# Products that nobody reads on TensorE, from the first router's search to the attention stage

## The chip, the cores and the metric

The kernel runs on one core of one Trainium2 chip. The metric is the device time of one execution in microseconds. Before the change three runs gave 2144.35, 2140.17 and 2142.94 us, median 2142.94 us. The change is judged by the time of the changed kernel against that.

## The reference

The program is a small language-model tower of two layers. For this case only the front of layer 0 matters: tokens are embedded, mixed by a recurrence, normalised, and then a router with 4 experts picks, per sequence and expert, the 256 of 512 tokens with the highest probability. The picks set which bands of columns each token uses in the attention and feed-forward layer behind it.

```python
    h = _L0_tok_ref(x, L0_tok_W)
    h = h + _L0_attn_ref(_layernorm(h, axis=-1), ...)          # recurrence
    h = h + _L0_ffn_ref(_layernorm(h, axis=-1), ...)           # router, attention, MLP
    ...
def _L0_ffn_ref(x, w_router, ...):
        cap = int(CAP_FACTOR * N)                              # 256 of 512
        logits = jnp.einsum('bnc,ec->bne', x, w_router)
        probs = jax.nn.softmax(logits, axis=-1)
        gate, idx = jax.lax.top_k(jnp.swapaxes(probs, 1, 2), cap)
        ...
        attn = jax.nn.softmax(jnp.einsum('bhqd,bhkd->bhqk', q, k) * scale, axis=-1)
```

## The kernel before, in words

The kernel is a chain of phases. Each phase is one block in which every engine has its own written-out program, and semaphores order them. Between two phases stands a barrier: each engine runs a DRAIN and then raises the barrier's semaphore (line 45), GpSimd releases all, SyncE clears the semaphores of the phase one after the other (line 53), and a second barrier (line 49) lets the next phase begin. No engine starts the next phase before the slowest has come to the barrier.

The first phase, `embed_and_route`, ends with the router. TensorE transposes the probabilities to 32 rows (8 sequences by 4 experts) of 512 tokens (line 636). VectorE copies them (line 504) and searches the 256th largest value of each row bit by bit, in `kth_largest`: 30 steps, each a comparison with a count over 512 columns (line 146), a decision (line 148) and the new candidate (line 150), with a drain behind each. TensorE has nothing to do meanwhile; its next instruction waits for `taken_ready`. VectorE then marks the ties and forms the two rows of taken tokens (lines 508 to 519), TensorE transposes them in 8 small matmuls (line 641), and VectorE spreads them into the tile `bands` (lines 526 and 528). That is the phase's last work.

The next phase, `moe_attention_ffn`, begins for GpSimd with the scaling of `y` by `bands` (line 910). TensorE's first work is the transposes of `y` (line 1110, 8 matmuls, two groups of four, each read out by ScalarE at line 1300), then three tiles of queries and keys (line 1120) and six tiles of the MLP (line 1135), each two calls of 512 columns in f32, then the values (line 1127). Only then come the row maxima of the attention (line 1145), which need `qT` and `c_kT`; these are loaded through DRAM by SyncE's queue (lines 853, 863 and 866) after VectorE has split each tile of queries and keys into three bf16 parts (lines 955 to 965). VectorE gets to the first split behind a memset of one row of `c_kT` (line 1068). The row maxima then alternate between TensorE and VectorE (line 975).

Of the kernel before, what the change touches and what calls it, by code (L numbers as in the profile page):

```python
# [5 lines left out]
ALU = mybir.AluOpType  # L6
# [128 lines left out]
CAP0 = T // 2  # L135
BANDS = ((0, 24), (24, 48), (48, 96), (96, 192))
TOP_BIT = 29
QUARTS = (TOP_BIT + 1) // 2

def kth_largest(dve, scores, cand, drop, count, mark, k):

    dve.memset(cand[:, :], 1 << TOP_BIT)
    dve.drain()
    for b in range(TOP_BIT, -1, -1):
        dve.tensor_scalar(mark, scores, cand[:, :].bitcast(F32), 0.0, ALU.is_ge, ALU.add, accum_out=count[:, :])
        dve.drain()
        dve.tensor_scalar(drop[:, :], count[:, :], float(k), float(1 << b), ALU.is_lt, ALU.mult)
        dve.drain()
        dve.scalar_tensor_tensor(out=cand[:, :], in0=cand[:, :], scalar=(1 << b) >> 1, in1=drop[:, :],  # L150
                                 op0=ALU.bitwise_or, op1=ALU.bitwise_xor)
        dve.drain()

# [44 lines left out]
def embed_and_route(kit, a, x1, bands, dealt, moe, work, spare):  # L199
# [6 lines left out]
    with kit.phase() as ctx:  # L206
# [29 lines left out]
        x1T = sb("b_xT", [P, 2, 2, T])  # L236
# [3 lines left out]
        bits = sb("bits", [R, 1], I32)  # L240
        drop = sb("drop", [R, 1], I32)
        count = sb("count", [R, 1])
        room = sb("room", [R, 1])
        ps_w = ps("a_ps_w", [P, BANKS_A, T])
        ps_o = ps("a_ps_o", [P, 4, T])
# [5 lines left out]
        score, mark, tie = (pnum[0:R, i, 0:T] for i in range(3))  # L251
# [8 lines left out]
            "a_small_in a_w_loaded a_rows_ready a_folded a_zeroed a_cleared a_var_ready a_rstd_ready a_xn_ready a_w_psum "  # L260
            "a_w_read a_met a_gaps_ready a_exps_ready a_z_ready a_out_psum a_h_done a_x1_ready a_den_ready a_logit_psum "
            "a_logit_read")
        shifted, exp_ready, probs_ready, score_psum, taken_ready, taken_psum = kit.sems(
            "b_shifted b_exp_ready b_probs_ready b_score_psum b_taken_ready b_taken_psum")
        moe_in, y_var, y_rstd, y_norm, y_scaled = kit.sems("a_moe_in a_y_var a_y_rstd a_y_norm a_y_scaled")
        rows_in = [kit.pool_dma_sem(f"a_rows_in{n}") for n in range(PAIRSEQ)]
        order = front_order()
# [69 lines left out]
        def _(dve):  # L337
# [165 lines left out]
            dve.wait_ge(score_psum, 1)  # L503
            dve.tensor_copy(score, ps_w[0:R, 0, :])
            dve.drain()
            kth_largest(dve, score, bits, drop, count, mark, CAP0)
            kth = bits[:, :].bitcast(F32)
            dve.tensor_scalar(mark, score, kth, 0.0, ALU.is_gt, ALU.add, accum_out=count[:, :])
            dve.tensor_scalar(tie, score, kth, None, ALU.is_equal)
# [22 lines left out]
        def _(pe):  # L532
# [102 lines left out]
            for j in range(J):  # L635
                last = pe.transpose(ps_s[:, j, :], prob_rows[:, j].rearrange("p b e -> p (b e)"), kit.ident[:, :])
            last.then_inc(score_psum, 1)
            pe.wait_ge(taken_ready, 1)
            for w in range(2):
                for j in range(J):  # L640
                    last = pe.transpose(ps_b[:, w, j, :], taken[:, w, j * P:(j + 1) * P], kit.ident[0:R, 0:R])
            last.then_inc(taken_psum, 1)

        @block.scalar
        def _(act):
# [2284 lines left out]
def lm_tower(nc, a, out_rows):  # L2930
    out = out_rows.rearrange("(b p) c -> p b c", p=P)
    dealt = nc.dram_tensor("dealt", (SLOTS, CX), F32, kind="Internal").ap()
    spread = nc.dram_tensor("spread", (G3, P, 3, T), BF16, kind="Internal").ap()
    with ExitStack() as ctx:
        kit = Kit(nc, ctx)
        setup_constants(kit)
        if PHASES > 1:
            ssm = SsmInputs(tile_maker(nc, ctx))
            with ExitStack() as layer:
                sb = tile_maker(nc, layer)  # L2940
                x1 = sb("x1", [P, NB, C])
                bands = sb("bands", [P, 2, NB, EXPERTS0])
                moe = MoeInputs(sb)
                embed_and_route(kit, a, x1, bands, dealt, moe, ssm.xm, ssm.w_in)
                moe_attention_ffn(kit, a, x1, bands, moe, ssm, spread)
        if PHASES > 2:
            state_space_block(kit, a, ssm)
        if PHASES > 3:
            experts_tower(kit, a, dealt, out, out_rows)
        else:  # L2950
            store_output(kit, out)
# [81 lines left out]
```

## Time and profile before

| what | before |
|---|---|
| median of three runs | 2142.94 us |
| the profiled execution, whole | 2141.69 us |
| its span, first to last instruction | 2139.8 us |
| mean granted TensorE clock | 0.939 |
| TensorE busy, matmuls | 1932.6 us, 90% of the span |
| VectorE busy | 1152.7 us, 54% |
| ScalarE busy | 739.9 us, 35% |
| GpSimd busy | 425.5 us, 20% |

The profiled execution is one run; it took 1.25 us less than the median and lies 1.89 us above its own span. Busy shares are means over stages with different limits, so they do not say what a change in one stage is worth.
### The profile page before, as it was taken

The page shows a single profiled execution, that of the slowest core. Times are in us where ns is not written, and L with a number is a line of the kernel's source. Part 1 is how long each engine was busy: PE and PEld are TensorE (multiplying, and loading weights), DVE is VectorE, ACT ScalarE, POOL GpSimd, SP SyncE. Part 2 cuts the span into 40 slices and gives each one's busy share as a digit, 9 for nine tenths or more (in the row PEclk, how much of TensorE's full clock was granted, in tenths as well). Part 3 has the DMA queues.
Part 4 walks back from the last instruction along what each step waited for, and adds up shares of the span by engine and source line. Part 5 has one row for each costly group of instructions (what it writes and reads, how often), then busy time and mean ns, then how long its engine had stood idle before and what let it go on. Part 6 is the DMA issues. An engine that isn't in the chain of part 4 may idle for free. (4 is left out here: it accounts for less than half of the span.)

```text
span 2139.8 us, 27931 instructions
## 1 busy us (share of the span) xinstructions
PE 1932.6 (90%) x10040; PEld 1216.2 (57%) x10048; DVE 1152.7 (54%) x2714; ACT 739.9 (35%) x1248; POOL 425.5 (20%) x521
## 2 busy tenths in 40 slices
PE   4997609999999999879999998799999999999997
PEld 2343503345444444445666665465558888888886
DVE  5798577676667665456877885347322222222221
ACT  1434002544555455544555553121111111111111
POOL 5200201120222021111111111100561222222222
PEclk9998557999999999978999999699999999999998
DMA  2610002211111112010000000200222322122221
GB/s 63 222 50 0 0 18 74 60 52 53 45 52 53 52 39 59 1 31 6 6 6 6 8 9 1 100 1 1 75 88 70 68 59 60 32 62 61 68 39 18
DMA packets 68746, 94.72 MB, mean 44 GB/s; under 512 B 15386, under 2 KB 57662, under 8 KB 66337
## 3 DMA queue, kind: packets, MB, share of 16 engines
q1 hardware_dynamic: 52482, 77.19, 11.2%
q0 software_dynamic: 16128, 15.76, 4.2%
q8 instruction: 80, 1.31, 0.3%
q14 instruction: 56, 0.46, 0.1%
HBM read 54.96 MB, written 39.47 MB: 44 GB/s over the span
## 5 line engine op out<-in xcount | busy, mean ns | idle before, releaser
L975 DVE TENSOR_REDUCE row_max<-c_ps_m 128x1 f32<-128x512 f32 x384 | 252.6, 686 | 114.2 <-PE c_ps_m L1145 108.9
L1323 ACT ACTIVATE e<-c_ps_s 128x512 f32<-128x512 f32 x384 | 216.6, 596 | 222.0 <-PE c_ps_s L1161 221.3
L2622 DVE TENSOR_TENSOR e_f<-e_ps_u,e_gate 128x512 f32<-128x512 f32 x120 | 83.0, 691 | 271.6 <-ACT e_gate L2904 179.1
L2423 POOL DMA_INDIRECT out<-m_o,m_row_of x80 | 125.7, 1572 | 280.7 <-issue 260.3
L2839 PE MATMUL e_ps_o<-m_w,e_f 128*128 128x192 f32 x960 | 162.6, 326 | 0.9 <-DVE e_f L2622 0.9
L2839 PEld LDWEIGHTS e_ps_o<-m_w,e_f 128*128 128x128 f32 x960 | 158.1, 190 | 3.3 <-DVE e_f L2622 1.3
L1145 PE MATMUL c_ps_m<-c_kT,qT 96*128 96x512 bf16 x384 | 150.2, 398 | 10.7 <-DVE row_max L975 10.6
L1161 PE MATMUL c_ps_s<-qT,c_kT 97*128 97x512 bf16 x384 | 145.4, 389 | 12.7 <-ACT e L1323 5.0
L2904 ACT ACTIVATE e_gate<-e_ps_g 128x512 f32<-128x512 f32 x120 | 71.7, 597 | 242.3 <-PE e_ps_g L2813 162.3
L2807 PE MATMUL e_ps_g<-m_xT,m_w 128*128 128x256 f32 x480 | 129.6, 392 | 1.0 <-DVE h L2454 1.0
L2807 PE MATMUL e_ps_u<-m_xT,m_w 128*128 128x256 f32 x480 | 123.2, 379 | 0.0
L2817 PE MATMUL e_ps_u<-m_xT,m_w 64*128 64x256 f32 x480 | 119.5, 389 | 0.0
L2813 PE MATMUL e_ps_g<-m_xT,m_w 64*128 64x256 f32 x480 | 119.5, 389 | 0.0
L1172 PE MATMUL c_ps_a<-e,v 128*32 128x512 f32 x768 | 106.3, 626 | 1.0 <-ACT e L1323 1.0
L2813 PEld LDWEIGHTS e_ps_g<-m_xT,m_w 64*128 64x128 f32 x480 | 85.0, 186 | 27.9 <-issue 19.9
L2807 PEld LDWEIGHTS e_ps_g<-m_xT,m_w 128*128 128x128 f32 x480 | 83.1, 190 | 28.4 <-issue 19.9
L2807 PEld LDWEIGHTS e_ps_u<-m_xT,m_w 128*128 128x128 f32 x480 | 91.2, 190 | 12.4
L1161 PEld LDWEIGHTS c_ps_s<-qT,c_kT 97*128 97x128 bf16 x384 | 36.5, 97 | 107.3 <-ACT e L1323 82.3
L2630 DVE TENSOR_SCALAR m_o<-e_ps_o,m_w_of 128x192 f32<-128x192 f32 x80 | 29.7, 413 | 125.8 <-PE e_ps_o L2839 125.8
L1135 PE MATMUL c_ps_w<-yT,w 96*128 96x512 f32 x192 | 90.3, 596 | 0.0
L2397 POOL DMA_INDIRECT dealt<-e_x,slot x64 | 62.5, 977 | 116.6 <-issue 111.0
L2817 PEld LDWEIGHTS e_ps_u<-m_xT,m_w 64*128 64x128 f32 x480 | 85.0, 186 | 0.0
(440 smaller groups left out, 3704.4 us busy)
## 6 DMA issues: line engine op xcount, KB each, us to landing
dealt<-x SPq DMA_DIRECT2D x8, 1290.0 KB, 15.0
m_x<-dealt SPq DMA_DIRECT2D x40, 258.0 KB, 2.7
spread<-parts SPq DMA_DIRECT2D x24, 384.0 KB, 2.3
qT<-spread SPq DMA_DIRECT2D x144, 64.0 KB, 2.5
c_kT<-spread SPq DMA_DIRECT2D x144, 64.0 KB, 2.4
m_w<-in_w13e SPq DMA_DIRECT2D x8, 1152.0 KB, 5.2
m_w<-in_w2e SPq DMA_DIRECT2D x8, 576.0 KB, 6.3
out<-h SPq DMA_DIRECT2D x8, 384.0 KB, 4.6
```

The lines of the kernel that those rows point to most:

```text
L975: dve.tensor_reduce(row_max[:, n // J, n % J:n % J + 1], ps_m[:, n % 2, :], AX_X, ALU.max)\
L1135: last = pe.matmul(bank(key), w1[0:CH + c, c, m * P:(m + 1) * P], yT[0:CH + c, c, :], start=c == 0, stop=c == 1)
L1145: pe.matmul(ps_m[:, n % 2, :], qT[0:STACK, h, j * P:(j + 1) * P], kT[0:STACK, h, :], start=True, stop=True).then_inc(m_psum, 1)
L1161: pe.matmul(ps_s[:, n % 2, :], kT[:, h, kc * P:(kc + 1) * P], qT[:, h, :], start=True, stop=True).then_inc(s_psum, 1)
L1172: last = pe.matmul(ps_a[32 * i:32 * i + 32, :], v[:, t % 2, kc, 4 * g + i, :], e[:, (4 * grp + i) % LIVE_E, :], start=kc == 0, stop=kc == ...
L1323: act.activation(e[:, n % LIVE_E, :], ps_s[:, n % 2, :], ACT.Exp, scale=QSCALE).then_inc(e_ready, 1)
L2423: pool.indirect_dma_start(out=out_rows, out_offset=bass.IndirectOffsetOnAxis(ap=row_of[:, n % 2, r:r + 1], axis=0), in_=o[:, n % 2, r, :], ...
L2622: dve.tensor_tensor(fe[:, n % 2, 2 * i:2 * i + 2, :], ps_ue[:, q % 2], gate_e[:, q % 2], ALU.mult)\
L2807: last = pe.matmul(dst[:, q % 2, k, :], w13e[:, u, w, here[k]], xeT[:, b, 0, :], start=first and k == 0, stop=not first and k == 1, skip_g ...
L2813: g_last = pe.matmul(ps_ge[:, q % 2, k, :], w13e[0:HALF, u, 2, here[k]], xeT[0:HALF, b, 1, :], start=first and k == 0, stop=not first and ...
L2817: u_last = pe.matmul(ps_ue[:, q % 2, k, :], w13e[HALF:P, u, 2, here[k]], xeT[HALF:P, b, 1, :], start=first and k == 0, stop=not first and ...
L2839: last = pe.matmul(ps_oe[:, b, r, 0:C], fe[:, b, m, r * P:(r + 1) * P], w2e[:, u, m, :], start=m == 0, stop=m == IT - 1)
```

## The change

Each step of the search now raises a new semaphore, `step`, from its last VectorE instruction. TensorE gets work that writes to the free tile `ps_o`, which nobody reads afterwards: at each of the 30 steps one product of the identity with 512 columns of `x1T`, f32, and six at the last step; and six more behind the transposes of the taken rows, before TensorE's end of the phase. The phase has one semaphore more to clear.

```diff
-def kth_largest(dve, scores, cand, drop, count, mark, k):
+def kth_largest(dve, scores, cand, drop, count, mark, k, step):
...
         dve.scalar_tensor_tensor(out=cand[:, :], in0=cand[:, :], scalar=(1 << b) >> 1, in1=drop[:, :],
-                                 op0=ALU.bitwise_or, op1=ALU.bitwise_xor)
+                                 op0=ALU.bitwise_or, op1=ALU.bitwise_xor).then_inc(step, 1)
...
             last.then_inc(score_psum, 1)
+            for n in range(TOP_BIT + 1):
+                pe.wait_ge(step, n + 1)
+                for i in range(6 if n == TOP_BIT else 1):
+                    pe.matmul(ps_o[:, i % 4, :], kit.ident[:, :], x1T[:, 0, 0, :], start=True, stop=True)
             pe.wait_ge(taken_ready, 1)
             for w in range(2):
                 for j in range(J):
                     last = pe.transpose(ps_b[:, w, j, :], taken[:, w, j * P:(j + 1) * P], kit.ident[0:R, 0:R])
             last.then_inc(taken_psum, 1)
+            for i in range(6):
+                pe.matmul(ps_o[:, i % 4, :], kit.ident[:, :], x1T[:, 0, 0, :], start=True, stop=True)
```

TensorE's instructions of the kernel before, from the transposes of the probabilities to the first transposes of `y`. `a_ps_w` and `a_ps_o` are PSUM tiles of the first phase, `c_ps_w` one of the second, `qden` holds the taken rows; each row is one form with its count.

```order
373 L636 MATMUL a_ps_w<-ident,fresh 32x128 [waits b_probs_ready,a_w_read]
374 L636 MATMUL a_ps_w<-ident,fresh 32x128 x3
375 L641 MATMUL a_ps_w<-ident,qden 128x32 [waits b_taken_ready]
376 L641 MATMUL a_ps_w<-ident,qden 128x32 x7
377 L45 UNCONDITIONAL_BRANCH
378 L1098 UNCONDITIONAL_BRANCH [waits barrier_Pool_Activation_PE_DVE_SP_release]
379 L1110 MATMUL c_ps_w<-ident,y 96x128 [waits c_y_ready]
```

In it TensorE goes from one wait straight to the next, and the 8 transposes are the last thing before the barrier. The same stretch of TensorE's program in the changed kernel, where `b_xT` is the tile `x1T` and lines behind the change stand 4 to 6 further:

```order
373 L636 MATMUL a_ps_w<-ident,fresh 32x128 [waits b_probs_ready,a_w_read]
374 L636 MATMUL a_ps_w<-ident,fresh 32x128 x3
375 L641 MATMUL a_ps_o<-b_xT,ident 128x512 [waits b_step] x30
376 L641 MATMUL a_ps_o<-b_xT,ident 128x512 x5
377 L645 MATMUL a_ps_w<-ident,qden 128x32 [waits b_taken_ready]
378 L645 MATMUL a_ps_w<-ident,qden 128x32 x7
379 L648 MATMUL a_ps_o<-b_xT,ident 128x512 x6
380 L45 UNCONDITIONAL_BRANCH
381 L1104 UNCONDITIONAL_BRANCH [waits barrier_Pool_Activation_PE_DVE_SP_release]
382 L1116 MATMUL c_ps_w<-ident,y 96x128 [waits c_y_ready]
```

35 products now stand ahead of the transposes of the taken rows, 30 of them behind a wait of their own, and six between those transposes and the barrier. The order on the other engines is as it was.

## Rows read from the trace of the kernel before

**Rows 1.** The page: span, and granted clock in 40 slices.
```profile
span 2139.8 us, 27931 instructions
PEclk9998557999999999978999999699999999999998
```
**Rows 2.** Timeline, VectorE, search, first and last of 30 steps (start, duration, engine, line).
```profile
266.39 0.73 DVE L146 TENSOR_SCALAR_CACHE_REDUCE pnum<-pnum,bits 32x512 f32<-32x512 f32 x1
...
303.29 0.73 DVE L146 TENSOR_SCALAR_CACHE_REDUCE pnum<-pnum,bits 32x512 f32<-32x512 f32 x1
...
304.32 0.15 DVE L150 SCALAR_TENSOR_TENSOR bits<-bits,drop 32x1 int32<-32x1 int32 x1
```
**Rows 3.** Timeline, from the taken rows to the next phase.
```profile
309.80 1.06 PE L641 MATMUL a_ps_w<-ident,qden 32*128 32x32 f32 x8 [44.38 <-DVE qden L518]
...
314.85 1.93 POOL L910 TENSOR_TENSOR y<-y,bands 128x96 f32<-128x96 f32 x4 [64.27 <-POOLq L49]
...
316.97 1.94 PE L1110 MATMUL c_ps_w<-ident,y 128*96 128x128 f32 x8 [6.11 <-POOL y L911]
```
**Rows 4.** Barrier, lines 45 and 53: count, shortest/median/longest ns, first to last start.
```profile
L45 PEldq DRAIN  x1: 1088/1088/1088, 309.8 to 309.8; - x1
L45 DVEq DRAIN  x1: 19/19/19, 312.5 to 312.5; - x1
...
L53 SPq EVENT_SEMAPHORE_RANGE_CLEAR  x32: 25/30/39, 312.7 to 314.5; - x32
```
**Rows 5.** End of the attention phase: TensorE's last matmuls (timeline), its DRAIN (line 45).
```profile
917.30 0.81 PE L1209 MATMUL c_ps_w<-w_att,xaT 96*128 96x192 f32 x4
...
L45 PEldq DRAIN  x1: 3117/3117/3117, 915.0 to 915.0; - x1
```
**Rows 6.** Pauses of TensorE: windows (busy us and counts, clock, DMA), one timeline row.
```profile
39.20:43.88 4.68, 0.00 (x0) 0.00 (x0) 4.38 (x18) 1.08 (x2) 3.27 (x4) 0.94 0.00 0
...
43.88 2.82 PE L544 MATMUL a_ps_w<-ident,xn 128*128 128x128 f32 x12 [4.70 <-DVE xn L129]
...
46.80:50.00 3.20, 3.20 (x8) 1.16 (x7) 3.03 (x4) 0.54 (x1) 2.59 (x3) 1.00 0.30 53
...
147.66:149.43 1.77, 0.01 (x1) 0.04 (x1) 1.61 (x2) 1.77 (x4) 0.00 (x0) 1.00 0.07 30
...
918.12:923.11 4.99, 0.00 (x0) 0.03 (x1) 1.88 (x6) 0.02 (x1) 0.00 (x0) 0.75 0.01 2
```
**Rows 7.** Window of the attention phase's first 512-column matmuls.
```profile
319.60:326.65 7.05, 7.05 (x9) 2.92 (x10) 6.70 (x4) 1.25 (x1) 0.00 (x0) 0.50 0.00 0
```
**Rows 8.** Weight loads of neighbouring matmuls (timeline); all matmuls of line 1135.
```profile
323.18 0.34 PEld L1120 LDWEIGHTS c_ps_w<-yT,w 96*128 96x128 f32 x1 [0.52 <-issue]
...
324.03 0.34 PEld L1120 LDWEIGHTS c_ps_w<-yT,w 97*128 97x128 f32 x1 [0.52 <-issue]
...
L1135 PE MATMUL c_ps_w<-yT,w x24: 590/592/687, 328.3 to 338.3; 96*128 96x512 f32 x12, 97*128 97x512 f32 x12
```
**Rows 9.** Ahead of the row maxima (timeline), and landing times (page, last number).
```profile
319.77 5.18 DVE L1068 MEMSET c_kT<- 1x6144 bf16 x1 [1.32 <-issue]
...
336.51 0.43 SPq L866 DMA_DIRECT2D c_kT<-spread  x1
...
341.37 0.59 PE L1145 MATMUL c_ps_m<-c_kT,qT 96*128 96x512 bf16 x2
...
c_kT<-spread SPq DMA_DIRECT2D x144, 64.0 KB, 2.4
```
**Rows 10.** Timeline, VectorE: line 957 raises a semaphore, 955 does not; drains between.
```profile
324.96 0.69 DVE L955 CAST parts<-c_ps_w 128x512 bf16<-128x512 f32 x1
325.73 0.69 DVE L957 TENSOR_TENSOR rest<-c_ps_w,parts 128x512 f32<-128x512 f32 x1
...
326.51 0.43 DVE L963 CAST parts<-rest 128x512 bf16<-128x512 f32 x1
```
**Rows 11.** Windows of the first row maxima.
```profile
343.80:347.10 3.30, 2.26 (x6) 0.55 (x6) 3.30 (x6) 0.00 (x0) 0.00 (x0) 1.00 0.52 141
347.20:350.00 2.80, 2.42 (x4) 0.42 (x4) 2.59 (x5) 0.00 (x0) 0.00 (x0) 0.50 0.45 130
```

More of the change, by code:

```diff
@@ L262, in embed_and_route @@
             "a_logit_read")
-        shifted, exp_ready, probs_ready, score_psum, taken_ready, taken_psum = kit.sems(
-            "b_shifted b_exp_ready b_probs_ready b_score_psum b_taken_ready b_taken_psum")
+        step, shifted, exp_ready, probs_ready, score_psum, taken_ready, taken_psum = kit.sems(
+            "b_step b_shifted b_exp_ready b_probs_ready b_score_psum b_taken_ready b_taken_psum")
         moe_in, y_var, y_rstd, y_norm, y_scaled = kit.sems("a_moe_in a_y_var a_y_rstd a_y_norm a_y_scaled")
@@ L505, in _ @@
             dve.drain()
-            kth_largest(dve, score, bits, drop, count, mark, CAP0)
+            kth_largest(dve, score, bits, drop, count, mark, CAP0, step)
             kth = bits[:, :].bitcast(F32)
```

## The prediction

> **What bounds the kernel now.** I read the page first. Its clock row is lowest, at 5, in the fifth and sixth slice (214 to 321 us), and the sixth is where the change works [rows 1]. Then I read the timeline from the search on. The search is VectorE's alone: 30 steps, from 266.39 to 303.29 in 29 intervals, so 1.27 us each, the last ending at 304.32 + 0.15 = 304.47 us [rows 2]. TensorE sits idle for 44.38 us until the taken rows are there, does its 8 transposes in 1.06 us, and idles again for 6.11 us [rows 3]. Nothing that TensorE does before 309.8 is waited for, so the phase's end is set by VectorE, and a faster TensorE can gain at most the transposes there.
>
> The view of the barrier shows how the phase ends. VectorE's DRAIN at 312.5 us takes 19 ns and is the last to arrive; the next phase starts at 314.85 [rows 3, 4]. TensorE's DRAIN begins at 309.8, before its transposes are through, and lasts 1088 ns, to 310.90, which is where the last of them ends (309.80 + 1.06 = 310.86).
>
> In the next phase TensorE does work that is waited for. Its 512-column matmuls begin at 319.60 and run at the granted clock 0.50 until 326.65 [rows 7], 1.2 GHz, start to start 324.03 - 323.18 = 0.85 us; behind that they are (338.3 - 328.3) / 23 = 0.435 us apart [rows 8], 2.4 GHz. The first row maximum starts at 341.37 [rows 9], right behind TensorE's own queue, so what this stretch saves or loses goes to the end, up to the point where another wait is later: the loads for the maxima, the last issued at 336.51 and landing some 2.4 us later, at 338.9 [rows 9]. These loads hang on VectorE's splits, which begin only behind the 5.18 us memset (to 324.95), so they do not come earlier with a faster TensorE. The margin is 341.37 - 338.9 = 2.5 us.
>
> **The search with products.** One f32 product of 512 columns is two matmuls in the trace: line 1135 makes 6 x 2 = 12 calls and has 24 rows [rows 8]. It takes 2 x 0.85 = 1.70 us at half clock and 2 x 0.435 = 0.87 us at full. At half clock TensorE falls behind the 1.27 us steps and works without a pause; at full clock it catches up and is idle for 0.40 us in each step. VectorE never waits for it. The last step releases six products: 12 x 0.435 = 5.22 us from 304.47, so to 309.69, and the taken rows come at 309.80 [rows 3]. So nothing is late there, at full clock.
>
> The search itself gains nothing. Its price is the semaphore: an instruction that raises one ends at 325.73 + 0.69 = 326.42 and the next starts at 326.51, a gap of 0.09 us, and behind one that raises none the gap is 325.73 - 325.65 = 0.08 [rows 10]. Over 30 steps the difference is 0.3 us; bounds 0 and 0.6. It delays TensorE's end as much as VectorE's.
>
> **The end of the phase.** The transposes run at full clock: half of (1.06 - 0.29) / 7 = 0.11 us each, so 8 x 0.055 = 0.44 us, and VectorE gets them 0.4 us sooner. That gain is covered, because TensorE is now the last to arrive. Its six products are 12 x 0.435 = 5.22 us from 309.80 + 0.44 = 310.24, so to 315.46, with 0.16 us until the last one is through (a duration of 0.59 against a distance of 0.435 [rows 8]) and 0.05 for the DRAIN: 315.67. The barrier waited until 312.5. The delay is 3.17 us, with the 0.3 us of the search 3.47, and with one more clear of (314.5 - 312.7) / 31 = 0.06 us [rows 4] it is 3.5 us. Everything in the next phase hangs behind this barrier: GpSimd's scaling, SyncE's loads, VectorE's memset. Bounds: 3.2 if the semaphore is free, 3.8 if it costs double.
>
> **The clock after the barrier.** TensorE stands still from 315.6 to 316.97 + 3.5 = 320.5, 4.8 us. Of pauses in this trace, one of 4.68 us and one of 4.99 us each lost the full clock before they were over (means 0.94 and 0.75 inside them), and one of 1.77 us kept it [rows 6]. So the attention phase starts at half clock again. How long it stays there is open: before, 7.05 us of 512-column work [rows 7]; after the 4.68 us pause the clock was back some 2.9 us after work resumed, at 46.8 [rows 6]. In our case 2.6 us go by on transposes and a wait first (316.97 to 319.60), so the half-clocked 512-column work is between 0.3 and 7.05 us, and half the difference to 7.05 is saved: 0 to 3.4 us, cut to 2.5 by the loads. The nearest row is the same stretch before, which gives 0. I take 1.0, a little toward the other end.
>
> The Trainium skill has a rule on this: TensorE: Matmul & The Clock Gate, Part 4: PE-mode transpose, says that transposes do not count as busy work for the clock. By that rule the transposes at the head of the attention phase would bring nothing back, and the sum would be the full 3.5 us. The trace disagrees in one place: 12 transposes, from 43.88 to 46.70, were nearly all that TensorE had done since its pause when it had full clock again at 46.8 [rows 6]. By that row the saving of 1.0 us can stand.
>
> **Sum.** + 3.5 us at the barrier - 1.0 us of half clock = + 2.5 us. Against the profiled execution, 2141.69 us, that is 2144.2; that execution is 1.25 us below the median of its kernel, so against the median, 2142.94, it is 2145.4 us, 0.12% more. The sum's own range is + 0.7 (3.2 - 2.5) to + 3.8: 2143.6 to 2146.7.
>
> **Rivals.**
> - The barrier is not held, and the clock survives. Were TensorE's DRAIN past its products at once, the barrier would fall at 312.5 as before, the products would end at 315.6, 1.3 us before the next work, and the attention phase would begin at full clock. It then saves 7.05 / 2 = 3.5 us, cut to 2.5 by the loads, less 0.36 for semaphore and clear: - 2.2 us. If the row maxima behind it, which ran at 0.50 from 347.2 on [rows 11], keep full clock too, some 18 of them gain up to 0.1 us each, in all - 4.0. Its time is about 2139.9. It decides at the DRAIN: against it stand 1088 ns on the 1.06 us of transposes [rows 4], and 3117 ns from 915.0 to 918.1, just as the last matmuls end at 917.30 + 0.81 = 918.11 [rows 5]. The Trainium skill, VectorE: DVE Perf Modes, The DRAIN you can't avoid, has the DRAINs of preamble and postamble as some 12 ns constant on all engines; by that rule this rival would hold, and here the trace disagrees, with 1088 ns.
> - The clock holds through the pause, or comes back at once. Then the saving is the full 2.5 us: + 1.0, 2143.9 us. The 1.77 us pause speaks for it, the two longer ones against.
> - TensorE loses the clock during the search and comes late. Spaced work can do that: the row maxima, a matmul every 0.6 us, had the full clock until 347.1 and half of it after [rows 11]. The products leave gaps of 0.40 us in 1.27. If the fall hits the last steps, the six products take up to 10.4 us instead of 5.2, and the taken rows wait up to 5.1 us; with half of that, 2.5, on top of 3.5 it is 2149.0 us. Against it: whenever TensorE is at half clock here it has work without a pause, so it can win the clock back.
> - VectorE's search is slowed by TensorE's reading of SBUF. Nothing in the trace shows the pair; even 0.05 us in each of 30 comparisons is + 1.5: 2146.9 us.
> - The products do not bring the clock up at all. Then the 35 products take 35 x 1.70 = 59.5 us from 267.6, to 327, the taken rows wait 17 us, and the last six add 10: 2142.9 + 25 = about 2168 us. Against it stand 7.05 us of the same kind of work that did win the clock [rows 7].
>
> **How the numbers follow.** Forecast 0.60, DRAIN does not hold 0.11, clock holds 0.11, TensorE late 0.12, VectorE slowed 0.05, no clock 0.01. About 0.2% (4.3 us) is what a measurement of this kernel can tell from no change; the runs before spread over 4.2 us. Faster by over 0.2%, below 2138.7, is only the far end of the first rival: 0.06. Slower by over 0.2%, above 2147.2: most of TensorE late (0.09), half of VectorE slowed (0.03), the forecast's upper tail with the spread of runs (0.12), no clock: 0.25. Within: 0.69. The range for 8 in 10 takes in the clock-holds case with its spread and most of TensorE late: 2141.5 to 2149.0.
>
> **What would show it.** In the profile of the changed kernel: the granted clock at 1.00 from about 275 to 315 us; products two per step with gaps of 0.40 us; the 8 transposes right behind the taken rows; TensorE's DRAIN at line 45 the last to arrive, some 5.7 us long from about 310, where VectorE's now comes 3 us before it; GpSimd's line 910 at about 318.4 instead of 314.85; half clock at the attention phase's first matmuls; and the first row maximum at about 343.9. The prediction is wrong if the next phase starts at 315 (the DRAIN does not hold), if the first row maximum is earlier than 341.4, or if the taken rows find TensorE busy.

## The result, and the profile after

| | before | changed kernel |
|---|---|---|
| median, six runs of each on one chip | 2142.71 us | 2148.12 us |
| lowest to highest | 2140.17 to 2145.28 | 2143.42 to 2152.54 |
| ratio, with its 95% interval | | 1.0025 [1.0015, 1.0036] |
| the profiled execution, whole | 2141.69 us | 2143.42 us |
| mean granted TensorE clock | 0.939 | 0.95 |

The changed kernel is slower by 0.25%, 5.4 us, between 3.2 and 7.7 us by the interval. The forecast was + 2.5 us. The clock did rise, and none of it reached the end.

The page of the changed kernel, span and granted clock in 40 slices, against [rows 1]:

```profile
span 2141.7 us, 28096 instructions
PEclk9998597999999999978999999699999999999998
```

The sixth slice went from 5 to 9. The two spans can't be subtracted for the change alone: the search begins at 266.4 us before and at 264.8 after, and over all the profiled executions of this case it began anywhere from 264.8 to 271.4 us, for reasons that lie ahead of the change. So I measure from the search's first step to a landmark behind it, within one execution. The timeline of the changed kernel, from the search to the row maxima, against [rows 2, 3, 9]:

```profile
264.82 0.73 DVE L146 TENSOR_SCALAR_CACHE_REDUCE pnum<-pnum,bits 32x512 f32<-32x512 f32 x1
266.06 8.87 PE L641 MATMUL a_ps_o<-b_xT,ident 128*128 128x512 f32 x14 [2.21 <-DVE bits L150]
275.09 1.12 PE L641 MATMUL a_ps_o<-b_xT,ident 128*128 128x512 f32 x2 [0.17 <-DVE bits L150]
...
303.51 5.42 PE L641 MATMUL a_ps_o<-b_xT,ident 128*128 128x512 f32 x12 [0.17 <-DVE bits L150]
308.86 0.68 PE L645 MATMUL a_ps_w<-ident,qden 32*128 32x32 f32 x8
309.46 5.42 PE L648 MATMUL a_ps_o<-b_xT,ident 128*128 128x512 f32 x12
...
317.30 1.13 POOL L916 TENSOR_TENSOR y<-y,bands 128x96 f32<-128x96 f32 x3 [68.29 <-POOLq L49]
319.42 1.94 PE L1116 MATMUL c_ps_w<-ident,y 128*96 128x128 f32 x8 [4.54 <-POOL y L917]
322.22 5.18 DVE L1074 MEMSET c_kT<- 1x6144 bf16 x1 [1.32 <-issue]
333.48 0.69 DVE L963 TENSOR_TENSOR rest<-c_ps_w,parts 128x512 f32<-128x512 f32 x1
343.83 0.60 PE L1151 MATMUL c_ps_m<-c_kT,qT 96*128 96x512 bf16 x2
```

The first products run without a pause (14 matmuls in 8.87 us, at half clock until 270.5 us and at full clock behind it); from 275.09 they come two per step, 276.38 - 275.09 = 1.29 us apart, of which two matmuls at full clock fill 0.87: the gaps of 0.4 us that I had forecast (the row's 0.17 us counts from the modelled end). From the search's first step to GpSimd's first instruction of the next phase it was 314.85 - 266.39 = 48.46 us before [rows 2, 3]; now it is 317.30 - 264.82 = 52.48: + 4.02 us. From that instruction to the first row maximum it was 341.37 - 314.85 = 26.52 us [rows 3, 9]; now it is 343.83 - 317.30 = 26.53. That is the whole result: four microseconds late at the barrier, nothing back before the first row maximum. The 4.0 us lie inside the 3.2 to 7.7 us that were timed.

The barrier's instructions (count, shortest/median/longest ns, first to last start), against [rows 4]:

```profile
L45 PEldq DRAIN  x1: 5856/5856/5856, 309.0 to 309.0; - x1
L45 DVEq DRAIN  x1: 19/19/19, 311.2 to 311.2; - x1
...
L53 SPq EVENT_SEMAPHORE_RANGE_CLEAR  x33: 25/29/39, 315.1 to 317.0; - x33
```

TensorE's DRAIN lasts until 314.9 us, VectorE's is through at 311.2. The barrier is held for 3.7 us, and the clears follow as before, one more of them.

Windows of the changed kernel (busy us with instruction counts of PE, PEld, DVE, ACT, POOL and SP; then the granted clock and the share and number of DMA), against [rows 6, 7]:

```profile
270.60:302.00 31.40, 27.79 (x52) 7.57 (x50) 25.01 (x99) 0.00 (x0) 0.00 (x0) 1.00 0.00 0
...
314.90:319.40 4.50, 0.00 (x0) 0.00 (x0) 1.85 (x10) 0.00 (x0) 2.10 (x6) 0.88 0.17 29
319.40:322.05 2.65, 1.95 (x9) 1.57 (x9) 1.27 (x2) 1.23 (x3) 0.95 (x1) 0.50 0.89 307
322.05:328.56 6.51, 6.51 (x8) 2.85 (x9) 6.25 (x3) 1.25 (x1) 0.00 (x0) 0.50 0.01 0
328.60:343.80 15.20, 15.10 (x45) 7.77 (x44) 8.44 (x18) 4.87 (x7) 5.42 (x7) 1.00 0.48 154
```

The products kept the full clock for as long as they came. It was lost inside the pause at the barrier, and the attention phase's first matmuls ran at 0.50 again, as they did before [rows 7].

What the first matmuls wait for was in the trace of before all along. Its timeline inside the MLP tiles:

```profile
331.03 0.69 DVE L957 TENSOR_TENSOR rest<-c_ps_w,parts 128x512 f32<-128x512 f32 x1
331.77 0.30 PEld L1135 LDWEIGHTS c_ps_w<-yT,w 96*128 96x128 f32 x2 [0.66 <-DVE rest L957]
```

TensorE waits here for VectorE's third split to free a PSUM bank: the tiles of this stretch go round three banks, and the third MLP tile needs the one that the third tile of queries and keys still holds. From that split to the first row maximum it is 341.37 - 331.03 = 10.34 us before and 343.83 - 333.48 = 10.35 now. VectorE's splits stand behind its memset of 5.18 us [rows 9], which starts at a fixed distance from GpSimd's first instruction: 319.77 - 314.85 = 4.92 us before and 322.22 - 317.30 = 4.92 now. So does the third split: 331.03 - 314.85 = 16.18 and 333.48 - 317.30 = 16.18 us. A faster TensorE comes sooner to this wait and leaves it at the same time.

### The profile page after: what moved, and what is told of

It is laid out like the page before. It is cut to its first block and busy times, and to the rows that moved or that the text cites. A ratio compares the mean times of both kernels' runs of the same rounds, so it can differ in the third digit from the quotient of the medians.

```text
span 2141.7 us, 28096 instructions
## 1 busy us (share of the span) xinstructions
PE 1976.9 (92%) x10122; PEld 1231.6 (58%) x10130; DVE 1152.8 (54%) x2714; ACT 739.5 (35%) x1248; POOL 424.9 (20%) x521
```

## The experiments

Distances "from the search" run from the instruction ahead of the first step to the release of the barrier: 48.54 us before, 52.56 us in the changed kernel. The first row maximum is 26.61 us behind that release in both (26.52 behind GpSimd's first instruction). Both depend little on the chip; the whole time does: the kernel before took 2143.68 us at the median of its runs beside the first four experiments and beside the last one 2142.39 us, but 2187.24 and 2172.58 us on the two chips between, and the profiles put nearly all of that in the kernel's last stage (777.5 us on the first kind, 803 to 824 us there). Each ratio is against the kernel before on the same chip.

**The products of the search without the last six.** From the changed kernel:

```diff
             last.then_inc(taken_psum, 1)
-            for i in range(6):
-                pe.matmul(ps_o[:, i % 4, :], kit.ident[:, :], x1T[:, 0, 0, :], start=True, stop=True)
```

> The changed kernel without the six products behind the transposes of the taken rows; the 35 products in the search stay. Theory (the barrier is held by TensorE's DRAIN over the last six products): VectorE is last at the barrier again. Against the kernel before + 0.6 us for the 30 semaphores (the step took 1.293 us instead of 1.272 in the changed kernel), - 0.5 us for the full clock at the 8 transposes, + 0.06 for the clear, so + 0.2 us at the start of the attention phase, TensorE's DRAIN about 1 us or less, and about 2143 us; that is 3.8 us less than the changed kernel. Rival 1 (the cost lies in the search: semaphores, shared memory, or TensorE coming late): the time stays at about 2148. Rival 2 (the loss is a worse clock in the attention phase, not the barrier): also near 2148, with the attention phase starting as in the kernel before.

Measured: 2142.24 us, ratio 0.9988 [0.9979, 0.9997]. The barrier's DRAINs:

```profile
L45 PEldq DRAIN  x1: 768/768/768, 315.4 to 315.4; - x1
L45 DVEq DRAIN  x1: 19/19/19, 317.7 to 317.7; - x1
```

VectorE is the last to arrive again, and the release comes 48.82 us from the search, + 0.28 us. So 3.74 of the 4.02 us are the last six products. The ratio was lower than anything in the trace gives (its release is later, not sooner), so I ran the kernel again on another chip.

> The kernel without the last six products once more, since its first timing came out 1.4 us below the kernel before (ratio 0.9988, interval 0.9979 to 0.9997) where its profile shows the attention phase starting 0.3 us later against the search's start and everything behind it as long as before. Theory (the products in the search only cost their semaphores, and the first timing was luck of the draw): ratio 1.0001, between 0.9993 and 1.0010. Rival (full clock in the search gains something that the profile hides, 1 to 2 us): again 0.999 or less.

Measured: 2171.03 us, ratio 0.9996 [0.9978, 1.0013], release at 48.87 us. The median shows no dip this time, and the products of the search alone make no difference that can be measured; but this interval still holds the first ratio of 0.9988, so a gain of that size is not excluded by the times. The profiles show none.

**The last six products alone.** The kernel before with these behind its transposes (and the semaphore `step`, which nobody raises but which is cleared with the others, 0.06 us):

```diff
             last.then_inc(taken_psum, 1)
+            for i in range(6):
+                pe.matmul(ps_o[:, i % 4, :], kit.ident[:, :], x1T[:, 0, 0, :], start=True, stop=True)
```

> The kernel before with only the six products behind the transposes of the taken rows; no products and no semaphore in the search. Theory (the barrier waits for TensorE's products): they run at half clock, 12 matmuls x 0.85 = 10.2 us from 310.9, less if the clock rises on the way; the DRAIN ends 5 to 8.6 us after VectorE's, the attention phase starts that much later, and the time is 2148 to 2151.5 us. If the clock comes up during the tail, it ends nearer 5. Rival (a DRAIN that is past its products): the attention phase starts as before, at 314.8, and the time is 2143 us or less.

Measured: 2151.08 us, ratio 1.0027 [1.0018, 1.0037], between + 3.9 and + 7.9 us; the release comes 55.16 us from the search, + 6.62. The DRAINs, and the windows of the products:

```profile
L45 PEldq DRAIN  x1: 9030/9030/9030, 313.2 to 313.2; - x1
L45 DVEq DRAIN  x1: 19/19/19, 315.6 to 315.6; - x1
```

```profile
312.90:319.70 6.80, 6.78 (x15) 3.44 (x16) 1.30 (x8) 0.00 (x0) 0.00 (x0) 0.50 0.00 0
319.70:322.30 2.60, 2.48 (x6) 0.76 (x4) 0.00 (x0) 0.00 (x0) 0.00 (x0) 1.00 0.00 0
```

Without products in the search the same six run mostly at half clock, and the barrier pays all of it. The DRAIN follows the length of what is queued: 768, 5856 and 9030 ns for none, six fast and six slow products.

**The semaphore alone.** The changed kernel without any product, the 30 raises of `step` left in:

```diff
             last.then_inc(score_psum, 1)
-            for n in range(TOP_BIT + 1):
-                pe.wait_ge(step, n + 1)
-                for i in range(6 if n == TOP_BIT else 1):
-                    pe.matmul(ps_o[:, i % 4, :], kit.ident[:, :], x1T[:, 0, 0, :], start=True, stop=True)
...
-            for i in range(6):
-                pe.matmul(ps_o[:, i % 4, :], kit.ident[:, :], x1T[:, 0, 0, :], start=True, stop=True)
```

> The changed kernel without any of its products: only the semaphore raised at each of the 30 search steps, and its clear, stay. Theory: a step takes 1.293 us as in the changed kernel, instead of 1.272, so the search is 0.6 us longer and the time + 0.7 us, 2143.4. Rival (the longer step came from TensorE's products reading SBUF beside VectorE): the step is 1.272 us as before, and the time + 0.1 us.

Measured: 2144.37 us, ratio 1.0002 [0.9993, 1.0011]; release at 49.15 us, + 0.61. The comparisons of the search, grouped by line (busy us and mean ns of one, idle us just before them), in the kernel before, in this one and in the changed kernel:

```profile
L146 DVE TENSOR_SCALAR_CACHE_REDUCE pnum<-pnum,bits 32x512 f32<-32x512 f32 x30 | 22.0, 735 | 2.7
```

```profile
L146 DVE TENSOR_SCALAR_CACHE_REDUCE pnum<-pnum,bits 32x512 f32<-32x512 f32 x30 | 22.0, 735 | 3.2
```

```profile
L146 DVE TENSOR_SCALAR_CACHE_REDUCE pnum<-pnum,bits 32x512 f32<-32x512 f32 x30 | 22.1, 735 | 3.3
```

A step takes 1.2909 us here, 1.2913 in the changed kernel, 1.2724 before: the raise costs 0.019 us of a step, 0.56 us in all, with or without TensorE at work. One comparison takes 735 ns in all three, so TensorE's reading of SBUF does not slow VectorE by anything that can be seen. With products the release is 0.33 us sooner (+ 0.28), since the transposes then run at full clock.

**Products on both sides of the barrier.** The products of the search stay; behind the transposes 896 columns, which end when VectorE does, and two products of 512 columns that nobody reads as TensorE's first work of the attention phase:

```diff
-            for i in range(6):
-                pe.matmul(ps_o[:, i % 4, :], kit.ident[:, :], x1T[:, 0, 0, :], start=True, stop=True)
+            for i, n in enumerate((512, 384)):
+                pe.matmul(ps_o[:, i, 0:n], kit.ident[:, :], x1T[:, 0, 0, 0:n], start=True, stop=True)
...
+            for i in range(2):
+                pe.matmul(ps_s[:, i, :], kit.ident[:, :], x1[:, :, :].rearrange("p b c -> p (b c)")[:, 0:T],
+                          start=True, stop=True)
             for c in range(2):
                 y_transpose(0, c)
```

> The changed kernel with the six products behind the transposes cut to two that end with VectorE's work (512 and 384 columns, 1.5 us at full clock), and two products of 512 columns put at the head of the attention phase, where TensorE waits for y (1.7 us of the 2.1 us it waits). TensorE's longest pause is then the barrier itself, about 2.6 us, instead of about 5 us. Theory (a pause of that length may keep the full clock, as 1.77 us did and 3.2 us did not): the attention phase starts + 0.3 us after the kernel before and at full clock, the first row maximum comes up to 2.5 us earlier against the phase's start, bounded by the loads, and the time is about 2140.5. If the pause still costs the clock: the two products at the head take up to 3.4 us instead of 1.7 and delay the transposes of y by up to 1.3 us, time 2143 to 2144.5. Rival (TensorE's start of the attention phase is not what the phase waits for): the first row maximum stays 26.6 us behind the phase's start even at full clock, time 2143.

Measured: 2144.22 us, ratio 1.0002 [0.9993, 1.0011]. Windows around the barrier, and the timeline behind it:

```profile
315.70:318.10 2.40, 0.03 (x1) 0.00 (x0) 0.00 (x0) 0.00 (x0) 0.00 (x0) 1.00 0.00 0
318.20:319.40 1.20, 1.20 (x3) 0.61 (x4) 1.14 (x4) 0.00 (x0) 1.20 (x4) 1.00 0.13 17
319.50:322.80 3.30, 2.84 (x10) 1.69 (x8) 1.92 (x7) 1.01 (x2) 1.70 (x3) 0.50 0.75 194
322.90:344.60 21.70, 18.93 (x52) 9.23 (x53) 14.74 (x20) 6.23 (x9) 5.43 (x7) 1.00 0.39 120
```

```profile
323.03 5.43 PE L1126 MATMUL c_ps_w<-yT,w 96*128 96x512 f32 x12 [0.69 <-ACT yT L1309]
...
329.77 1.99 PE L1141 MATMUL c_ps_w<-yT,w 96*128 96x512 f32 x4 [1.31 <-DVE rest L963]
332.42 1.12 PE L1141 MATMUL c_ps_w<-yT,w 96*128 96x512 f32 x2 [0.67 <-DVE rest L963]
...
344.67 0.59 PE L1151 MATMUL c_ps_m<-c_kT,qT 96*128 96x512 bf16 x2
```

By this run my last step falls. Through a pause of 2.4 us the clock stayed at 1.00; it fell only at 319.5, for 3.4 us, and from 322.9 on all of the phase's 512-column work ran at full clock (12 matmuls in 5.43 us). But the first row maximum came 344.67 - 318.15 = 26.52 us behind GpSimd's first instruction (at 318.15), exactly as before. The time that TensorE saved became the 1.31 and 0.67 us of waiting for VectorE's splits.

**The memset behind the splits.** If VectorE is the gate, moving its memset out of the way must help the kernel before, with no product at all:

```diff
-            dve.memset(kT[STACK:STACK + 1, :, :], 1.0)
             for g in range(G3):
                 split_high(0, g)
                 split_low(g)
             norm_apply(1)
+            dve.memset(kT[STACK:STACK + 1, :, :], 1.0)
```

> The kernel before with one edit: VectorE's memset of one row of c_kT (5.18 us, ahead of its first split of the queries and keys) stands behind its norm of sequence 1, where VectorE waits for TensorE's values. No products. New theory (in all of before, changed and the first four kernels the first row maximum stood 26.61 us behind the phase's start, whatever the clock did: the MLP tiles wait for banks that VectorE's splits free, and the splits wait for this memset): the wait for the splits goes, TensorE's own queue is what is left, and at half clock it is nearly as long (its queue was through the second MLP tile when the third split freed the bank), so the first row maximum comes 0 to 1.5 us earlier, more if the clock happens to rise early, and the time is 2142 to 2143.5. Rival (TensorE's queue never mattered and the loads for the row maxima are the bound): they come up to 2 us earlier with the splits, also with half clock, and the time is 2141.5.

Measured: 2187.06 us, ratio 0.9995 [0.997, 1.002]; GpSimd's first instruction and the first row maximum:

```profile
314.96 1.93 POOL L910 TENSOR_TENSOR y<-y,bands 128x96 f32<-128x96 f32 x4 [64.27 <-POOLq L49]
...
340.42 0.59 PE L1145 MATMUL c_ps_m<-c_kT,qT 96*128 96x512 bf16 x2
```

340.42 - 314.96 = 25.46 us: 1.06 us less. The gate moved: VectorE's first split now waits for TensorE's first tile (it starts at 323.52 us), and that tile runs at half clock, and the third split starts 329.59 - 314.96 = 14.63 us behind GpSimd's first instruction, 1.55 us sooner than before. Of that 0.49 us is lost again further on, because the memset now stands ahead of VectorE's copies of the values, and TensorE waits for these:

```profile
334.06 5.18 DVE L1072 MEMSET c_kT<- 1x6144 bf16 x1 [1.33 <-issue]
...
339.25 0.89 DVE L970 COPY v<-c_ps_w 128x192 f32<-128x192 f32 x3
339.66 0.92 PE L1127 MATMUL c_ps_w<-w,yT 96*128 96x192 f32 x4 [0.22 <-DVE v L970]
```

The time could not tell on this chip, so I repeated it.

> The kernel before with the moved memset alone, once more. Its first timing (ratio 0.9995, interval 0.997 to 1.002) was too wide to say whether the memset or the bridge makes the gain of the kernel that has both (0.9969 and 0.9974). In the profile the moved memset alone brought the first row maximum 1.1 us forward and the end of the attention phase 3.0 us, the kernel with both 3.7 and 3.0 to 3.5 us. Theory (nearly all of the gain is the memset): ratio 0.9982 to 0.9990. Rival (the bridge is what counts in the timing): 0.9995 or more.

Measured: 2140.04 us, ratio 0.9992 [0.9981, 1.0003]. The first maximum comes 1.06 us sooner again, and the attention phase is 2.9 us shorter (605.35 against 608.24 us). Little of that is the 1.06 us: among the row maxima, 53 us into the phase, only 0.2 us of it is left (the row maxima lost the full clock earlier in the phase than before, and for 20.5 us instead of 17.1), and the rest comes in two stretches of 3.4 us, at 381 and 450 us, where the kernel before ran at half clock and this one at full (1.2 and 1.6 us). Nothing or up to 4 us: the time leaves it open.

**Both together.** The products on both sides of the barrier and the moved memset, in one kernel:

> The bridge kernel (products in the search, two behind the transposes, two at the head of the attention phase) with the memset of c_kT moved as in the kernel with the memset alone. New theory: with the gate at VectorE gone, TensorE's full clock now counts: the first row maximum comes 2.5 to 4 us earlier than 26.6 us behind the phase's start, and the time is 2140.5 to 2142 where the bridge alone gave no gain. That is more than the sum of the two edits alone. Rival (the clock does not matter in this stretch at all): the gain is that of the memset alone plus nothing.

Measured: 2182.03 us, ratio 0.9979 [0.9957, 1.0000]. The first row maximum comes 24.06 us behind the release, 2.55 us sooner than before: 1.06 by the memset alone, 0 by the clock alone, 2.55 by both. GpSimd's first instruction and the first row maximum:

```profile
318.15 1.93 POOL L916 TENSOR_TENSOR y<-y,bands 128x96 f32<-128x96 f32 x4 [64.62 <-POOLq L49]
...
342.11 0.60 PE L1151 MATMUL c_ps_m<-c_kT,qT 96*128 96x512 bf16 x2
```

The clock fell here too, from 319.3 to 322.7 us, as with the products on both sides alone.

**And only the last 14 steps of the search.** From that kernel, the semaphore and the product in 14 steps instead of 30:

```diff
-        dve.scalar_tensor_tensor(out=cand[:, :], in0=cand[:, :], scalar=(1 << b) >> 1, in1=drop[:, :],
-                                 op0=ALU.bitwise_or, op1=ALU.bitwise_xor).then_inc(step, 1)
+        last = dve.scalar_tensor_tensor(out=cand[:, :], in0=cand[:, :], scalar=(1 << b) >> 1, in1=drop[:, :],
+                                        op0=ALU.bitwise_or, op1=ALU.bitwise_xor)
+        if b < 14:
+            last.then_inc(step, 1)
...
-            for n in range(TOP_BIT + 1):
+            for n in range(14):
                 pe.wait_ge(step, n + 1)
-                for i in range(6 if n == TOP_BIT else 1):
+                for i in range(6 if n == 13 else 1):
```

> The kernel with bridge and moved memset, but only the last 14 of the 30 search steps raise the semaphore and get a product. Theory: each raised semaphore costs 0.019 us of search, so 16 fewer give 0.3 us; the clock comes up within the last 14 steps (18 us), before the six products of the last step. The phase starts 0.3 us earlier than in that kernel against the search's start, and the time is 0.3 us less. Rival: 18 us are too short for TensorE to have caught up, the taken rows find it busy, and the time is 1 to 3 us more.

Measured: 2180.13 us, ratio 0.9969 [0.9947, 0.9991]. Windows around the barrier:

```profile
317.20:319.50 2.30, 0.00 (x0) 0.00 (x0) 0.00 (x0) 0.00 (x0) 0.00 (x0) 1.00 0.00 0
319.50:323.00 3.50, 3.03 (x12) 1.54 (x12) 3.00 (x11) 0.68 (x2) 3.05 (x6) 1.00 0.58 158
323.00:342.40 19.40, 18.72 (x53) 9.37 (x54) 14.68 (x21) 6.55 (x9) 5.42 (x7) 1.00 0.48 146
```

The clock is full from 297.3 us, inside the search, to 345.1 us, among the row maxima. The first maximum is 22.94 us behind the release, 3.67 us sooner than before, and the release itself is only 0.04 us late: 14 raises cost 0.27 us and the faster transposes give about as much back. By its time this kernel is faster than the kernel before and than the changed one; against the one with 30 steps the difference of 1.9 us is within the noise. Its repeat, on a third chip:

> The kernel with bridge, moved memset and products in the last 14 search steps once more, beside the kernel without the last six products, for a second timing of it. Theory (the first row maximum 22.9 to 24.1 us behind the phase's start instead of 26.61, some 3.1 us of it left at the phase's end): ratio 0.9985 to 0.9988. Rival (the 0.9969 of its first timing was all its own): 0.997 again.

Measured: 2166.16 us, ratio 0.9974 [0.9956, 0.9991]; first maximum at 22.95 us. Faster twice, each time by an interval that is clear of 1. The profiles account for about half of it: the attention phase takes 605.17 and 604.60 us against 608.24, and the release is 0.04 and 0.13 us late, so 3.0 and 3.5 us, where the medians are 7.1 and 6.4 us apart. The intervals include the smaller gain; whether there is more is open.

**The changed kernel again, and its tail halved.** The changed kernel unaltered beside the three above:

> The changed kernel once more, unaltered, beside the others on one chip. Theory (barrier + 4.0 us, nothing given back behind it): the attention phase starts 52.5 us after the search's start, the first row maximum 26.61 us behind that, and the time is 4.0 us above the kernel before, 2147.7 on the median. Rival (the first result of + 5.4 us holds a second loss of 1.4 us): again + 5 or more, and a stretch behind the first row maximum that is longer than in the kernel before.

Measured: 2188.90 us, ratio 1.0023 [0.9998, 1.0048]; release at 52.56 us, first maximum at 26.61, both as in its first profile. Then three products behind the transposes instead of six, one run:

> The changed kernel with three products instead of six behind the transposes of the taken rows. Theory (the barrier waits for the last product, 2 x 0.43 us each at full clock): TensorE's DRAIN ends 3 x 0.86 = 2.6 us sooner against the search's start, 47.7 us behind it instead of 50.3, still 1.1 us behind VectorE's, and the attention phase starts 50.0 us behind the search's start instead of 52.6. Rival (a fixed cost of having work in flight at the barrier): it stays near 52.6, or falls to 48.8 at once.

```profile
L45 PEldq DRAIN  x1: 3472/3472/3472, 312.4 to 312.4; - x1
L45 DVEq DRAIN  x1: 19/19/19, 314.7 to 314.7; - x1
```

Release at 49.97 us, + 1.43; TensorE's DRAIN ends 1.14 us behind VectorE's. Against six products that is 2.59 us for six matmuls, 0.43 us each. (The one run took 2170.70 us; that says nothing about differences of this size.) The barrier's price has the form of a maximum: nothing while TensorE is through before VectorE (+ 0.28 us with no tail, + 0.37 with 896 columns), from there on every matmul in full.

## Why the prediction was right and wrong

- **The barrier is held: right.** It was the argument against the strongest rival, the DRAIN that does not hold, and 768, 3472, 5856 and 9030 ns settle it. The rival's rule in the Trainium skill (VectorE: DVE Perf Modes, The DRAIN you can't avoid) gives some 12 ns, constant, for the DRAINs of preamble and postamble. At the end of this block VectorE's DRAIN is nearly that short and constant, 19 ns in every run; TensorE's is neither.
- **Its size: predicted + 3.5, measured + 4.0 us.** The semaphore was taken at 0.3 us and measures 0.57 us (30 x 0.019), almost the bound of 0.6. I had read it from gaps that the profile gives to 0.01 us on rows of another shape [rows 10]. The last six products start 0.60 us behind the first transpose (309.46 - 308.86), not 0.44. The rest is within 0.1 us. Both together put the measured 4.0 above the bound of 3.8 that I had given.
- **The clock is lost in the pause: right.** Full from 270.5 to 318.3 us, lost before work resumed at 319.42. The rivals "the clock holds", "no clock" and "TensorE late" are out: the six products of the last step begin at 303.51 and take 12 x 0.435 = 5.2 us, to 308.7, and the transposes begin at 308.86, 44.04 us behind the search's first step; before it was 309.80 - 266.39 = 43.41 us, and the difference of 0.63 is the semaphore's 0.57 within 0.06.
- **The clock gives 1.0 us back: wrong, 0.** The step that failed is that the first row maximum starts "right behind TensorE's own queue, so what this stretch saves or loses goes to the end". I tested the loads as the next limit and found 2.5 us of room, but not the banks: I took the memset as holding back only the loads, though the same splits free the PSUM banks that the MLP tiles need. The distance of 26.61 us did not change by 0.01 us with the clock at half (before, changed), at full for all the 512-column work (products on both sides), or with the half clock placed elsewhere (the last six alone). It changed by 1.06 us with the memset, and by 2.55 and 3.67 us with both. Of the half-clocked work I had also hoped that it would be shorter; it was about as long, 6.5 us against 7.05. That would have been worth 0.27 us, and the wait for the third split took it: TensorE's weight loads stand idle 0.93 us there instead of 0.66.
- **VectorE slowed by TensorE: refuted,** 735 ns with and without.
- **The range: held by luck.** 2148.12 us lies above the sum's own range, which ended at 2146.7, and inside the wide one, to 2149.0, only by the room that was left for a TensorE that comes late; it did not. The outcome above 2147.2 us had been given a chance of 0.25. The first row maximum at 343.83 us, forecast at 343.9, is luck too: against the search's first step it is 4.0 us late and not 2.5, and the search happened to begin 1.6 us earlier.
- **Corrected sum:** + 0.57 us for the semaphore, - 0.31 for the transposes, by which VectorE ends sooner, + 3.70 from VectorE's end to TensorE's, + 0.06 for one more clear: + 4.02 us. The forecast's 2145.4 us was 2.7 below the measured median, of which 1.5 us are these terms. The rest is not explained: the timed + 5.4 us includes 4.0 in its interval, and so does the repeat (+ 5 us, between - 0.4 and + 10.5). A second loss of about 1.4 us is neither shown nor excluded. The profiled execution, 2143.42 us, is the fastest of the six, so its trace can't show what the others lost; in it, and in the repeat's, the attention phase is about as long as before (607.57 and 608.50 us, against 608.24).

## What to carry to other kernels

Work that only keeps an engine warm must end before the slowest engine reaches the barrier: what is queued beyond that point is paid matmul by matmul. Before a faster engine is priced, look inside its own stretch for a wait on another engine, also one of under a microsecond; if the distance between two landmarks stays the same to 0.01 us while the clock changes, the gate is elsewhere. Here, at the first row maximum, the clock was worth nothing alone, the memset 1.06 us, and both 2.55 us, or 3.67 where the clock stayed full throughout. And a gain at one landmark need not reach the next: of the memset's 1.06 us, 0.2 was left 26 us later.

## What the runs showed of the hardware

- Pauses of 2.3 and 2.4 us at the barrier kept the full clock in the four profiles of kernels with products on both sides; pauses of 4.5 us and more lost it. Yet in the two with products in 30 steps the clock fell for 3.4 us just after such a pause (at 319.5 and 319.3 us), and in the two with 14 it did not. The kernel before has the same behind a pause of 3.2 us: full from 124.57 to 127.77, half from 128.7 to 132.1. And in the repeat without the last six products it fell as early as 1.6 us after TensorE's last transpose (312.98 to 314.62 us). What decides is open.
- Raising a semaphore from a short VectorE instruction between drains cost 0.019 us (a step of 1.2724 us became 1.2909).
- TensorE's DRAIN at the end of a block lasted until its last queued matmul was through, 768 to 9030 ns; VectorE's took 19 ns each time.
- TensorE's matmuls with 0.87 us of work in every 1.29 us held the full clock for 28 us, from 275.1 to 303.5 us, where denser work followed.
- Chips differ by 1 to 2% on the same kernel (2143, 2172 and 2187 us), mostly in one stage.
